# Second attention: key and value of a token tile made together with tokens on the partitions, key's sums by ScalarE's accumulator, query tiles first in a group

## The reference

```
q = (x @ Wq.T)  32 heads of 128;   k, v = (x @ Wk.T), (x @ Wv.T)  8 heads of 128
q = q / sqrt(mean(q*q) + 1e-6) * q_norm_w;   k = k / sqrt(mean(k*k) + 1e-6) * k_norm_w
scores = q . k / sqrt(128) + slope[head] * (t - s), masked where t > s   (4 query heads per key head)
out = softmax(scores) @ v;   x = x + out @ Wo.T
```

## Time and profile before

| | us |
|---|---|
| median of 3 runs | 1809.84 (1807.38 to 1810.34) |
| profiled execution, its own time | 1811.87 |
| its span, first to last instruction | 1810.2 |
| PE busy, PEld busy | 1736.5, 1443.1 |
| DVE, ACT, POOL busy | 1295.3, 877.6, 787.8 |

### The profile page before, as it was taken

One profiled execution on the slowest core, in us unless ns is written; L12 is line 12 of the kernel. 1 busy time (PEld: TensorE's weight loads), 2 busy tenths in 40 slices (PEclk: granted clock), 3 DMA queues, 4 the chain that ended last, 5 costly groups with the idle time before them and its releaser, 6 DMA issues.

```text
span 1810.2 us, 28744 instructions
## 1 busy us (share of the span) xinstructions
PE 1736.5 (96%) x8864; PEld 1443.1 (80%) x8864; DVE 1295.3 (72%) x2317; ACT 877.6 (48%) x2288; POOL 787.8 (44%) x924
## 2 busy tenths in 40 slices
PE   8999999999999987997999999999999996899999
PEld 7888888888888877876788888888888885678887
DVE  5788788788878774434777778777878777656555
ACT  3656665665566453222544444444444444544543
POOL 5334436253543542343545445454546333254442
PEclk9999999999999998999999999999999999999999
DMA  4122212221222310000100000000001002022111
GB/s 145 36 70 75 71 57 93 79 66 64 74 65 70 115 53 11 1 29 5 31 30 29 29 29 29 29 29 29 29 29 31 22 9 73 12 66 62 58 58 47
DMA packets 47711, 87.77 MB, mean 48 GB/s; under 512 B 6576, under 2 KB 6576, under 8 KB 47536
## 3 DMA queue, kind: packets, MB, share of 16 engines
q1 hardware_dynamic: 47664, 87.19, 15.2%
HBM read 77.73 MB, written 9.44 MB: 48 GB/s over the span
## 4 chain that ended last, share of the span: by engine, by line
PE 56%; DVE 5%; ACT 3%; POOL 2%; issue 1%; DMA 0%; POOLq 0%; DVEq 0%; ACTq 0%; SPq 0%
PE ring L316 10%; PE ring L318 10%; PE ring L317 10%; PE scores L316 3%; PE scores L318 3%; PE scores L317 3%; PE turned L316 3%; PE turned L318 3%; PE turned L317 3%; PE scores L712 2%; PE turned L798 2%; PE turned L791 1%; PE turned L762 1%; PE turned L763 1%; PE turned L784 1%
## 5 line engine op out<-in xcount | busy, mean ns | idle before, releaser
L316 PE MATMUL ring<-xt_hi,w_lo 128*128 128x512 f32 x768 | 304.6, 397 | 3.9 <-DVE qt_lo L941 1.5
L317 PE MATMUL ring<-xt_lo,w_hi 128*128 128x512 f32 x768 | 303.8, 396 | 0.0
L318 PE MATMUL ring<-xt_hi,w_hi 128*128 128x512 f32 x768 | 303.8, 396 | 0.0
L316 PE MATMUL ring<-wd_hi,ot_lo 128*128 128x512 f32 x512 | 207.5, 405 | 8.8 <-DVE xt_lo L494 3.6
L813 ACT CAST pt_hi<-turned 128x512 fp32r<-128x512 f32 x192 | 100.7, 592 | 234.1 <-PE turned L791 232.4
L317 PE MATMUL ring<-wd_lo,ot_hi 128*128 128x512 f32 x512 | 202.6, 396 | 0.0
L318 PE MATMUL ring<-wd_hi,ot_hi 128*128 128x512 f32 x512 | 202.6, 396 | 0.0
L574 POOL TENSOR_SCALAR sq_hi<-sq 128x512 fp32r<-128x512 f32 x80 | 55.2, 690 | 284.7 <-ACT sq L839 266.3
L316 PEld LDWEIGHTS ring<-xt_hi,w_lo 128*128 128x128 f32 x768 | 145.2, 189 | 36.6 <-DVE qt_lo L941 2.0
L318 PEld LDWEIGHTS ring<-xt_hi,w_hi 128*128 128x128 f32 x768 | 144.8, 189 | 34.7
L317 PEld LDWEIGHTS ring<-xt_lo,w_hi 128*128 128x128 f32 x768 | 144.9, 189 | 31.4
(11 more groups left out here) (247 smaller groups left out, 4410.0 us busy)
## 6 DMA issues: line engine op xcount, KB each, us to landing
w_raw<-w_attn_dram SPq DMA_DIRECT2D x96, 256.0 KB, 3.1
wd_raw<-w_dense_dram SPq DMA_DIRECT2D x64, 256.0 KB, 2.7
code_early<-codes_dram SPq DMA_DIRECT2D x28, 256.0 KB, 2.8
absmax_early<-absmax_dram SPq DMA_DIRECT2D x56, 128.0 KB, 3.0
kept_dram<-deq_early SPq DMA_DIRECT2D x28, 256.0 KB, 2.0
stage<-kept_dram SPq DMA_DIRECT2D x28, 256.0 KB, 2.7
code_late<-codes_dram SPq DMA_DIRECT2D x14, 256.0 KB, 2.6
absmax_late<-absmax_dram SPq DMA_DIRECT2D x28, 128.0 KB, 2.9
```

Source lines behind the costliest of these rows:

```text
L316: nc.tensor.matmul(o, l_lo, r_hi, start=start, stop=False)
L317: nc.tensor.matmul(o, l_hi, r_lo, start=False, stop=False)
L318: return nc.tensor.matmul(o, l_hi, r_hi, start=False, stop=stop)
```

## The change

In the second attention alone, K and V are no longer projected as weight-stationary tiles. A step `("kv", j, half, ahead)` takes two token tiles of 128 as the stationary operand (xt_hi, xt_lo) and the K and V weights of the group side by side (256 columns) as the moving one: 24 matmuls of 256 columns into one ring bank, with tokens on the partitions for both. ScalarE squares the key part of each token tile with a sum by its accumulator (`k_sum`), and copies the value part to v_hi; VectorE writes the key's mean square, copies the key to `k_tok` and writes v_lo. Steps `k_rms` and `v_turn` are gone. In `roots` VectorE multiplies `k_tok` by the root; `k_norm` waits for that (`s_k_scaled`) and transposes `k_tok`, and VectorE applies the norm weights while writing `keys`, which GpSimd splits as before. The sums of squares of the queries are 4 rows instead of 5.

The order: slots 1 and 3 make Q0, Q1, Q2; slots 2 and 0 make Q3, kv 0, kv 1. `q_rms` of Q0 and Q1 stands before the third tile (it stood behind `out` 1), `q_rms` of Q2 and Q3 before `out` 0. The weights are refilled in the order Q0, Q1, Q2, Q3, K, V; Q0, Q1, Q2 are held back in slot 3, and K and V are split behind kv 1 of half 1. The squares of the key are no longer split by GpSimd.

```diff
+REFILL = [[K, Q0, Q1, Q2, Q3, V], [Q0, Q1, Q2, Q3, K, V]]
@@ slot_steps
-        tiles = [K, Q0, Q1] if b in (1, 3) else [Q2, Q3, V]
+        tiles = [Q0, Q1, Q2] if b in (1, 3) else [Q3]
...
+    t += [("kv", j, half, ahead) for j in range(2)] if rms and tiles == [Q3] else []
...
-    s += [("k_rms", half)] if rms and tiles[0] == K else []
     s += [("roots_done",)] if roots else []
+    s += [("q_rms", half, 0)] if rms and tiles[0] == Q0 else []
+    s += t[2:3] + [("normalise", 1)] + ([] if rms else [("dq_lines", 1), ("dq_top", 0)])
+    s += [("q_rms", half, 1)] if rms and tiles[0] == Q3 else []
+    s += [("out", 0)] + ([("v_turn", half)] if tiles[-1] == V else [])
     s += [("k_norm", 1 if b == 1 else 0)] if roots else []
-    s += [("w_next", X) for X in (Q0, Q1)] if rms and b == 3 else []
+    s += [("w_next", X) for X in (Q0, Q1, Q2)] if rms and b == 3 else []
...
-        s += [("out", 1), ("q_rms", half, 0 if tiles[0] == K else 1)]
+        s += [("out", 1)]
@@ first_slot_steps
+        s = [("tile", Q3, 1, 0)] + softmax[0] + [("w_next", Q0)] + softmax[1] + [("kv", 0, 1, 0), ("w_next", Q1)]
+        s += softmax[2] + [("q_rms", 1, 1), ("kv", 1, 1, 0), ("normalise", 1)]
+        return s + [("w_next", X) for X in (Q2, Q3, K, V)] + [("transpose",)]
@@ lead_steps
+        s = [("norm_stats", [3]), ("tile", Q0, 0, 0), ("norm_root", [3], "dve"), ("norm_write", 3, "dve")]
+        s += [("tile", Q1, 0, 0), ("kv", 0, 0, 0), ("q_rms", 0, 0), ("tile", Q2, 0, 0), ("tile", Q3, 0, 0)]
+        s += [("norm_turn", 3), ("kv", 1, 0, 0), ("q_rms", 0, 1), ("q_rms_turn", 0), ("tile", Q0, 1, 0)]
+        return s + [("roots", 0), ("tile", Q1, 1, 0), ("k_norm", 0), ("q_rms", 1, 0), ("tile", Q2, 1, 0)]
@@ pe_steps
+                    elif step[0] == "kv":
...
+                        for t in range(2):
+                            at = slice(half * HALF + (2 * j + t) * P, half * HALF + (2 * j + t + 1) * P)
+                            for c in range(DC):
+                                ins = mm3(tile[:, t, :], xt_hi[:, c, at], xt_lo[:, c, at], w_hi[:, K:V + 1:V - K, c, :],
+                                          w_lo[:, K:V + 1:V - K, c, :], start=c == 0, stop=c == DC - 1)
...
-                        pe_sq.up(3 if pair == 0 else 2)
+                        pe_sq.up(2)
                         pe.wait_ge(s_sq_split, pe_sq.value())
...
-                        pe.wait_ge(s_roots, pe_roots.value())
+                        pe.wait_ge(s_k_scaled, pe_roots.value())
                         for q in range(HALF // P):
-                            ins = nc.tensor.matmul(tile[:, q * P:(q + 1) * P],
-                                                   root[:, step[1], q, HEADS:ROWS].to_broadcast([P, P]),
-                                                   ident[:, :], start=True, stop=True)
+                            ins = nc.tensor.transpose(tile[:, q * P:(q + 1) * P], k_tok[:, q, :], ident[:, :])
@@ act_steps
+                        act.wait_ge(s_ring_hi, act_hi.value())
+                        for t in range(2):
+                            nc.scalar.activation(k_square[:, t, :], tile[:, t, 0, :], ACT.Square,
+                                                 accum_out=k_sum[:, 2 * j + t:2 * j + t + 1])
+                        at = slice(4 * half + 2 * j, 4 * half + 2 * j + 2)
+                        act_ring_hi(nc.scalar.copy(v_hi[:, at, :], tile[:, :, 1, :]))
@@ dve_steps
+                        nc.vector.tensor_scalar(ms[:, at, HEADS], k_sum[:, at], 1.0 / HD, RMS_EPS, ALU.mult, ALU.add)
+                        nc.vector.tensor_copy(k_tok[:, at, :], tile[:, :, 0, :])
...
+                        dve_ring_free(nc.vector.tensor_tensor(v_lo[:, at, :], tile[:, :, 1, :],
+                                                              as_f32(v_hi[:, at, :]), ALU.subtract))
...  (in roots, behind the last Newton step)
+                        nc.vector.tensor_tensor(k_tok[:, :, :], k_tok[:, :, :],
+                                                root[:, half, :, HEADS:ROWS].to_broadcast([P, HALF // P, HD]),
+                                                ALU.mult).then_inc(s_k_scaled, 1)
...
-                        keys = k_raw[:, step[1], :]
-                        dve_ring_free(nc.vector.tensor_tensor(keys, keys, tile, ALU.mult))
+                        dve_ring_free(nc.vector.tensor_scalar(keys[:, :], tile, norm_cols[:, 2:3], None, ALU.mult))
@@ pool_steps
+                    elif step[0] == "kv" and step[1:3] == (1, 1) and refill and not held(b, K):
+                        pool.wait_ge(s_ring_full, pool_ring.value())
+                        for X in (K, V):
+                            pool_split_w(pool, X, REFILL[layer].index(X))
@@ sp_load_w
                 sp.wait_ge(s_w, sp_w.value() - 2)
+                hold(sp)
             sp_w.up()
-            sp.dma_start(w_raw[:, X % 3, :], w_attn[group, X, :, :]).then_inc(s_w_raw[X % 3], 16)
+            sp.dma_start(w_raw[:, at % 3, :], w_attn[group, X, :, :]).then_inc(s_w_raw[at % 3], 16)
```

More of the change, by code:

```diff
@@ L194, in tail_steps @@
     return s
-RING_STEPS = ("tile", "k_rms", "v_turn", "q_rms", "q_rms_turn", "k_norm", "out")
+RING_STEPS = ("tile", "kv", "v_turn", "q_rms", "q_rms_turn", "k_norm", "out")
 LEAD_STEPS = ("lead_write", "lead_turn", "warm")
@@ L606, in attention @@
                 sq_lo = sb("sq_lo", [P, 2, HALF], F32R, scope)
-                k_raw = sb("k_raw", [P, 2, HALF], F32, scope)
+                k_tok = sb("k_tok", [P, HALF // P, HD], F32, scope)
+                k_sum = sb("k_sum", [P, HALF // P], F32, scope)
+                k_square = sb("k_square", [P, 2, HD], F32, scope)
+                keys = sb("keys", [P, HALF], F32, scope)
                 sumsq = xn
@@ L676, in dve_lead, with pe_weights @@
                                                 as_f32(xt_hi[:, :, at]), ALU.subtract).then_inc(s_lead_lo, 1)
+            def pe_weights(pe, X, g, ahead, b):
+                if rms and b is None:
+                    pe.wait_ge(s_w, WT * (GROUPS + 1))
+                else:
+                    pe.wait_ge(s_w, WT * (GROUPS * layer + g + ahead) + REFILL[layer].index(X) + 1)
             def pe_steps(pe, steps, g, b):
@@ L702, in pe_steps @@
                             v_at[0] = pe_ring.n
+                    elif step[0] == "kv":
+                        _, j, half, ahead = step
+                        tile = pe_ring_bank(pe).rearrange("p (t d) -> p t d", t=2)
+                        if half == 0 and j == 0:
+                            pe_weights(pe, V, g, ahead, b)
+                        for t in range(2):
[3 more added lines that the diff above has]
+                                          w_lo[:, K:V + 1:V - K, c, :], start=c == 0, stop=c == DC - 1)
+                        pe_ring_done(ins)
                     elif step[0] == "norm_turn":
@@ L746, in pe_steps @@
                         pe_ring_done(ins)
[L747 to L752, removed]
                     elif step[0] == "q_rms":
@@ L759, in pe_steps @@
                             h = 2 * pair + j
-                            part = (half + 1 + h) % 2
+                            part = h % 2
                             row = pick[:, P - h:2 * P - h]
@@ L853, in act_steps @@
                                                    tile.rearrange("p (t d) -> p t d", d=HD)))
-                    elif step[0] in ("k_rms", "q_rms", "q_rms_turn", "k_norm", "out"):
+                    elif step[0] == "kv":
+                        _, j, half, ahead = step
+                        tile = act_ring_tile(act).rearrange("p (t x d) -> p t x d", t=2, x=2)
+                        act.wait_ge(s_ring_hi, act_hi.value())
[4 more added lines that the diff above has]
+                        act_ring_hi(nc.scalar.copy(v_hi[:, at, :], tile[:, :, 1, :]))
+                    elif step[0] in ("q_rms", "q_rms_turn", "k_norm", "out"):
                         act_ring.take(side=step[0] != "out")
@@ L928, in dve_steps @@
                             dve_ring_free(nc.vector.tensor_copy(vt[:, :], tile))
-                        elif X == K and rms:
-                            tile = dve_ring_tile(dve)
-                            dve_sq.up()
-                            dve.wait_ge(s_sq, dve_sq.value())
-                            dve_ring_free(nc.vector.tensor_scalar(k_raw[:, half, :], tile, norm_cols[:, 2:3], None,
-                                                                  ALU.mult))
-                        else:
-                            if rms:
-                                dve_sq.up()
+                        else:
                             tile = dve_ring_tile(dve, after_hi=True)
@@ L1005, in pool_steps @@
                         pool_norm(pool, step)
-                    if step[0] in ("k_rms", "q_rms"):
+                    if step[0] == "q_rms":
                         squares_used[0] = pool_ring.n
@@ L1011, in pool_steps @@
                             pool_sq.up()
```

(2 more changed lines are left out.)

90 lines of the change are left out of this document (43 added, 47 removed).

## The result

The changed kernel takes 1828.84 us in the median of four runs (1826.29 to 1831.69), the kernel before 1809.64 beside it (1807.38 to 1810.34): ratio 1.0109, interval 1.0091 to 1.0127. The forecast was 1818.6 with a range to 1827: slower, as said, but by twice as much, and 1.8 us beyond the range.

A forecast was written before the change was run, and what follows sets the result against it. TensorE's issue order was taken as the bound. B slots -5.5, A slots +6.4 and +7.6, ends +0.3 gave +8.8 us: 1820.7 for the profiled execution, 1818.6 for the median, range 1803 to 1827.

The forecast's parts named there:

- Work saved: TensorE's work in the second attention: value transposes, key sums and fp32 key norm shrink or go; kv tiles cost slightly more.
- B slots: Slots 2 and 0, making Q3 and the two kv tiles: each 0.39 us shorter, 14 of them, -5.5 us.
- A slot: Slots 1 and 3, making Q0, Q1, Q2: each could be 1.01 us shorter if nothing waits.
- rival 4: Weight loads of the kv matmuls run in series, 24 more per half: 46 us, 1865; chance 0.01.
- New wait 1: A slots: query sums wait for GpSimd's split of Q1's squares, about 1 us in slot 3, 2.1 in slot 1.
- New wait 2: The scores behind each A slot wait for the split keys: 0.64 us each.
- Rival 1: The scores' wait for the split keys does not appear, as VectorE or GpSimd catch up: 8.4 us less, 1810; chance 0.19.
- rival 2: TensorE's saved work counts whole, splits and keys in time: 1790, or 1800 for half; chance 0.13 with its half.
- rival 3: Waits feed on each other, 0.5 us in each of 28 slots: 1832; chance 0.09.
- The A slots' sum: Seven slots 3 and the first slot 1 at 0.8 us (+6.4), plus six slots 1 at 1.27 (+7.6).
- the term for the six slots 1: Six slots 1 with output weights split in front: 1.27 us longer each, +7.6 us.
- Lead, first slot, end: Lead up to first scores -0.5 us (bounds -3 and +2), first slot 0, last slot 1 +0.8; ends +0.3.

The follow-up runs named there:

- experiment 7: Changed kernel with three pairs of split-square buffers, keys written over k_tok, and the sums of Q0 and Q1 behind the second output tile: 1800.23 us.
- experiment 1: Changed kernel with three pairs of split-square buffers instead of two, sums still early in the loop, lead's first sums ahead of its key turn: 1829.88 us.
- experiment 4: Changed kernel with the lead's last tile (Q2 of the second half) moved to the start of the first slot, loop unchanged: 1826.98 us.
- experiment 5: Changed kernel with Q2 of the second half moved into the first slot and the first half's roots ahead of Q0, loop unchanged: 1824.38 us.
- experiment 8: Kernel of experiment 7 with the lead's roots ahead of Q0, and Q2 of the second half plus the Q0 and Q1 sums in the first slot: 1792.08 us.
- experiment 2: Changed kernel with three pairs of split-square buffers and the sums of Q0 and Q1 moved behind the first output tile, ahead of the key turn: 1833.87 us.
- experiment 3: Changed kernel with only the key turn moved one step earlier, ahead of the first output tile: 1825.79 us.
- experiment 6: Changed kernel with three pairs of split-square buffers, keys written over k_tok, and the sums of Q0 and Q1 directly behind the third tile: 1809.02 us.

## Why the prediction came out as it did

- **Work saved: right.** B slots 20.76 to 20.80 for the forecast 20.8: -5.3 us over 14, forecast -5.5. Kv matmuls start every 0.12 us. The A slot's saving of 1.01, if nothing waited, is the 1.06 of experiment 7. The rule of the Trainium skill (TensorE: Matmul & The Clock Gate, Part 3, The mechanism), by which a weight load overlaps a matmul only where row groups differ, does not show here, and that section itself also names a load into the background weight buffer as one that is pulled ahead. Each of these matmuls has a load of its own over all rows and they still start every 0.12 us, so rival 4 is out.
- **New wait 1: right in place, cause and size.** 0.86 us in slot 3 (about 1 was said) and 1.86 to 2.17 in slot 1 of later turns (2.1).
- **New wait 2: right.** 0.6 us, 14 times. Rival 1 is out, rival 2 too (no A slot under 23 us), and rival 3: B slots have no idle TensorE.
- **The A slots' sum: too low by 2.9**, 16.9 for the forecast 14.0. Slots 3 came to +0.59 each (+4.1 over seven; +5.6 forecast). The four slots 1 of later turns at the full clock came to +1.09 to +1.34 (+1.26 forecast). The other two came to +2.67 and +2.89, the slow stretch adding 1.5 each, and the first slot 1 to +2.2 for the forecast 0.8: there transposes and scores ran slow up to 879.11, behind the first slot's 4.64 us wait for p. So the term for the six slots 1, forecast +7.6, was +10.5. In three other kernels with the same waits 3 to 4 of the six slots 1 are slow (experiments 1, 4, 5), and their loops are 1.3 to 3.9 us longer than the changed kernel's. I had priced the slow clock at one restart.
- **The step that failed: "Lead, first slot, end".** It said -0.5 for the lead with bounds -3 and +2, and first slot 0. Lead and first slot measured +4.6 and -1.6, so 3.0 for -0.5. Idle TensorE is 2.3 of the lead's 4.6 (11.47 us for 9.20) and busy time the other 2.3 (41.57 for 39.25), although the lead has less work. I had the key turn's wait for the scaled keys, but not its size (4.09 us; 1.39 before), not the 2.17 us wait behind it, and not that the matmuls between and behind them then run at 0.43 us each: the lead's clock is 0.84, that of before 0.93. By the forecast's 1.7 us of work saved, the slower clock cost some 4.0 here, an estimate (2.3 + 1.7). The first slot's -1.6 is in part luck: before, its clock was 0.81; in the change it is 0.89, and the slow stretch reaches into the loop's first slot 1 instead (0.93, before 1.00). The 2.17 comes from a rule of the code that I had overlooked: each list of steps starts by waiting for all ring tiles ahead of it, and the change put a fresh query tile right ahead of the first slot. Altering the lead and the head of the first slot alone brought medians 1.9 and 4.5 us lower in experiments 4 and 5, the first not clear of noise, and 8.2 in 8.
- **The forecast** was right in direction and in both waits, and 10.2 us short in the median. **The 11.0 us** by which the profiled execution exceeded my 1820.7 are 3.5 in lead and first slot, 2.9 in the A slots, 0.2 in the B slots, 0.4 in the last slots, and 4.0 before and behind the attention. No run here settles whether these last 4.0 are more than the spread between executions; that stays open.

## What to carry to other kernels

A step that depends on another engine's result is free only while enough other work stands between the two in the issue order: here 19 us of waits came of issuing four matmuls up to 2.2 us too early, and they went when the step moved 3 us back, behind work that needed nothing. When such a step is moved, look at both neighbours: two small steps that use one PSUM bank back to back turn one wait into another (experiments 2, 3 and 6). Where a late step needs one more buffer, try that before an order that frees the buffer early: here the third pair alone brought nothing (experiment 1), and the late sums came with it (experiments 6 and 7); no run has the late sums with two pairs.

## What the runs showed of the hardware

- TensorE's clock fell to its lower level behind idle times of about 2 us in some slots and not in others: of slots 1 with waits of 1.85 to 2.26 us, two of six in the changed kernel and three or four of six in three others (experiments 1, 4, 5) were 1.2 to 1.7 us longer, at a mean clock of 0.93 or 0.94. In the kernels whose longest wait in these slots was 0.7 and 1.0 us (experiments 7 and 6) no such slot is slow. What decides between the two at equal waits was not tried.
- A square with a sum on ScalarE is recorded as two instructions: 0.27 to 0.33 us for 128 columns (median 0.28) and 0.19 to 0.27 for reading the accumulator (median 0.21), over the 64 of the changed kernel. The two records overlap: in a row, one such pair starts 0.25 to 0.27 us after another (909.33 and 909.58; 914.08 and 914.35).
